# Second stage of a fused attention and gated-FFN kernel: weight jobs issued behind the loads, a semaphore each for queries, keys and V, and a new table of maxima with D1 in the tenth step

## Time and profile before

| | |
|---|---|
| median of 3 runs | 1126.77 us (1122.39 to 1134.81) |
| the profiled execution | 1119.51 us, span of its instructions 1117.7 us |
| busy in the span | PE 93%, DVE 84%, ACT 65%, POOL 42% |
| stage 2 | group 0 starts at 192.3 us, group 15 at 680.0 us, stage 3's first matmul at 709.2 us |

### The profile page before, as it was taken

How to read it: one execution, slowest core, us unless ns; L and a number is a source line. 1 busy time by engine, 2 the same in 40 slices (tenths; PEclk the granted TensorE clock), 3 DMA queues, 4 the chain that set the end, 5 groups by cost and what they waited for, 6 DMA issues and landing times. The chain is left out here.

```text
span 1117.7 us, 18980 instructions
## 1 busy us (share of the span) xinstructions
PE 1039.0 (93%) x6242; PEld 639.5 (57%) x6242; DVE 933.7 (84%) x2162; ACT 722.6 (65%) x1152; POOL 465.6 (42%) x554
## 2 busy tenths in 40 slices
PE   5999987998999999989999999899999999999995
PEld 4788764433344343433444333577778778777874
DVE  6778897887888787878889885579989998998896
ACT  3666655675767666666667668567747766774774
POOL 2566545221111111111121112039946864994686
PEclk9999999999999998999999999899999999999997
DMA  6254862543544544464454343100120011012001
GB/s 214 70 158 137 220 149 78 154 123 64 142 109 109 129 78 97 90 142 109 95 125 94 103 87 106 39 1 0 40 75 1 1 49 66 1 39 76 1 1 38
DMA packets 98584, 95.32 MB, mean 85 GB/s; under 512 B 28030, under 2 KB 80950, under 8 KB 98486
## 3 DMA queue, kind: packets, MB, share of 16 engines
q1 hardware_dynamic: 96854, 93.72, 32.7%
q10 hardware_dynamic: 1632, 0.39, 0.2%
HBM read 72.45 MB, written 21.23 MB: 84 GB/s over the span
## 5 line engine op out<-in xcount | busy, mean ns | idle before, releaser
L896 ACT ACTIVATE pr<-pair 128x1024 f32<-128x1024 f32 (+3 forms) x384 | 296.6, 813 | 168.1 <-PE pair L1017 90.7
L279 DVE CUSTOM_DVE_ANT_0 bank<-bank,sg 128x384 f32<-128x384 f32 (+3 forms) x488 | 231.4, 517 | 73.4 <-PE bank L289 72.1
L1538 PE MATMUL pair<-xc_lo,w_gu 128*128 128x512 f32 x448 | 182.6, 408 | 4.1 <-DVE xc_lo L1374 4.1
L1539 PE MATMUL pair<-xc_hi,w_gu 128*128 128x512 f32 x448 | 176.5, 394 | 0.0
L282 DVE TENSOR_REDUCE mx<-bank 128x1 f32<-128x512 f32 x240 | 150.5, 684 | 6.0 <-PE bank L289 3.7
L1386 DVE SCALAR_TENSOR_TENSOR gate<-pair,sgu,gate 128x512 f32<-128x512 f32 x168 | 124.5, 741 | 27.0 <-PE pair L1539 25.4
L1177 POOL TENSOR_TENSOR yt<-yt,tmp 128x512 f32<-128x512 f32 x96 | 124.2, 1314 | 0.0
L289 PE MATMUL bank<-ks,qs 108*128 108x512 bf16 (+3 forms) x384 | 116.2, 335 | 5.6 <-DMA ks<-in_krows 5.0
L1012 PE MATMUL pair<-s_sb,xin_c 111*128 111x512 bf16 (+3 forms) x384 | 97.8, 338 | 12.0 <-DMA s_sb<-dt 9.2
L289 PE MATMUL bank<-xin_c,s_sb 108*128 108x512 bf16 (+3 forms) x344 | 106.0, 341 | 3.1 <-DMA xin_c<-in_krows 3.0
L1012 PE MATMUL pair<-qs,ks 111*128 111x512 bf16 (+3 forms) x384 | 97.1, 337 | 12.7 <-DMA qs<-dt 11.0
(11 more groups left out here) (122 smaller groups left out, 2166.5 us busy)
## 6 DMA issues: line engine op xcount, KB each, us to landing
stk<-parts SPq DMA_DIRECT2D x16, 768.0 KB, 5.7
zst<-in_z_all SPq DMA_DIRECT2D x24, 448.0 KB, 4.0
sst<-in_w_all SPq DMA_DIRECT2D x24, 448.0 KB, 5.7
xin_c<-in_x SPq DMA_DIRECT2D x32, 256.0 KB, 3.3
s_sb<-stk SPq DMA_DIRECT2D x96, 64.0 KB
xin_c<-stk SPq DMA_DIRECT2D x96, 64.0 KB
qs<-stk SPq DMA_DIRECT2D x96, 64.0 KB
ks<-stk SPq DMA_DIRECT2D x96, 64.0 KB
```

Source lines behind the costliest of these rows:

```text
L279: dve.tensor_tensor_reduce(out=src, in0=src, in1=tri[:, 512 - w:512], scale=1.0, scalar=-3.0e38, op0=ALU.add, op1=ALU.max, accum_out=dst). ...
L896: act.activation(pr[e % 3][:, 2 * p:2 * p + 2, 0:w], pair[p][:, :, 0:w], ACT.Exp, scale=SCALE)\
L1538: pe.matmul(GB[j % 4], w, xc_lo[:, k, :], start=True, stop=False)
L1539: pe.matmul(GB[j % 4], w, xc_hi[:, k, :], start=False, stop=True).then_inc(gu_done, 1)
```

## The change

- SP: in both groups of a pair the job at the group's start is now job s (0 in even, 1 in odd groups), none in group 0. Job 2 is issued in odd groups, behind the load of half 1 and ahead of the load of half 0. ACT converts job 2 at step 2 of the next even group; that of the last pair after the last exponentials, and POOL finishes it after its last group.
- A load is split into 7 DMAs of keys and then 7 of queries, with semaphores `k_in`, `q_in` per slot and half. V has `v_in`, and PE waits for it at step 0 before `pv` of its own group.
- PE waits in the ring for keys of half 1 at the first "u" piece, queries of half 1 at the first early piece, keys of half 0 at the first early piece of the lower half, queries of half 0 at the first head piece.
- The table: 48 pieces, D0, D1, O0, O1 as before, in another order.
- ACT's copy of the upper output of a group waits until O0 of the group before has been transposed.

```diff
-        LOADS = (16 * 15, 16 * 14)
+        LOAD = 16 * 7
...
 PLAN (three rows to a step)
-            "4u 5u 3", "4u", "6u",
-            "5u 2", "3 2", "4u 3",
-            "7u", "7u 3", "2 7u",
-            "O0", "6u 4u", "2 6u",
-            "5u", "6u 7u", "5 4",
-            "6", "4 5", "D0 5",
-            "6", "7 6", "5u",
-            "4", "7", "5",
-            "7 7", "4 6", "",
-            "1", "O1 0", "0",
-            "D1 1", "", "0",
-            "", "1 1", "0",
+            "2 2", "2", "4u",
+            "2 6u", "3 3", "5u 7u",
+            "3 7u", "6u", "5u 5u",
+            "4", "3 7 4", "6u 4u",
+            "4u", "4 4 6", "7",
+            "D0 6", "5 7u", "6u",
+            "5", "7u 7", "5 6",
+            "", "", "4u 7",
+            "5u 5", "6", "O0",
+            "", "", "D1",
+            "1", "", "0 1",
+            "", "O1", "0 0 1 1 0",
...
 SyncE, a group
-                    if s == 1:
-                        half_job(ip, 2)
-                    if not last:
-                        half_job(*((ip, 1), (ip + 1, 0))[s])
+                    if i > 0:
+                        half_job(ip, s)
...
                         load(sp, i + 2, s, 1)
+                    if s == 1:
+                        half_job(ip, 2)
+                    if last is None:
                         sp.wait_ge(s_full[1], full(i, NSTEP - 1, 1))
-                        load(sp, i + 2, s, 0, values=False)
+                        load(sp, i + 2, s, 0)
...
 TensorE, ring
                         if x == of_kind["upper"][0]:
-                            pe.wait_ge(stk_in[1 - s][1], LOADS[1] * (i // 2 + 1 + s))
+                            pe.wait_ge(k_in[1 - s][1], loaded)
+                        if x == of_kind["early"][0]:
+                            pe.wait_ge(q_in[1 - s][1], loaded)
                         if x == of_kind["lower"][0]:
-                            pe.wait_ge(stk_in[1 - s][0], LOADS[0] * (i // 2 + 1 + s))
+                            pe.wait_ge(k_in[1 - s][0], loaded)
+                        if x == of_kind["head"][0]:
+                            pe.wait_ge(q_in[1 - s][0], loaded)
...
 ScalarE, a group
-                        if e == JOB1_AT and s == 1:
-                            convert(ip, 1)
+                        if e == JOB2_AT and s == 0 and i > 0:
+                            convert(ip - 1, 2)
                         if e == JOB_AT:
-                            convert(ip, (0, 2)[s])
+                            convert(ip, s)
```

More of the change, by code:

```diff
@@ L161, in build @@
                 of_hi, of_lo = zip(*[[sb_in(c2)(f"{name}{n}", [P, 512], F32R) for name in ("of_hi", "of_lo")] for n in (0, 1)])
-        stk_in = [[sem(f"stk_in{n}_{b}") for b in range(2)] for n in range(2)]
-        LOADS = (16 * 15, 16 * 14)
+        q_in = [[sem(f"q_in{n}_{b}") for b in range(2)] for n in range(2)]
+        k_in = [[sem(f"k_in{n}_{b}") for b in range(2)] for n in range(2)]
+        v_in = [sem(f"v_in{n}") for n in range(2)]
+        LOAD = 16 * 7
         def load_v(sp, i, s):
-            sp.dma_start(vs[s][:, :, :], vscr[i // GROUPS, :, :, i % GROUPS, :].rearrange("t p w -> p t w"))\
-              .then_inc(stk_in[s][0], 16)
@@ L171, in load, with load_q @@
-        def load(sp, i, s, b, values=True):
+            sp.dma_start(vs[s][:, :, :], vscr[i // GROUPS, :, :, i % GROUPS, :].rearrange("t p w -> p t w")).then_inc(v_in[s], 16)
+        def load_q(sp, i, s, b):
             cols = slice(b * 512, (b + 1) * 512)
[L175 to L181, removed]
@@ L182, in load @@
             g = i % GROUPS
+            src = stk[0, bass.ds(i // GROUPS, 1), bass.ds((i % 2) * 64, 64), bass.ds(g // 2, 1), :, :]\
+                .rearrange("a (j c) k w s -> w c (a j) (k s)", j=GH)
+            for r, part in enumerate((0, 1, 2, 0, 1, 0)):
+                sp.dma_start(qs[s][r * HD:(r + 1) * HD, b, :, :], src[part][:, :, cols]).then_inc(q_in[s][b], 16)
             sp.dma_start(qs[s][96:ROWS_MAX, b, :, :], qrows[bass.ds(g, 1), :, :, cols].rearrange("a p j s -> (a p) j s"))\
-              .then_inc(stk_in[s][b], 16)
+              .then_inc(q_in[s][b], 16)
@@ L185, in load, with load_k @@
+        def load_k(sp, i, s, b):
+            cols = slice(b * 512, (b + 1) * 512)
+            g = i % GROUPS
+            src = stk[1, bass.ds(i // GROUPS, 1), bass.ds((i % 2) * 64, 64), bass.ds(g // 2, 1), :, :]\
+                .rearrange("a (j c) k w s -> w c (a j) (k s)", j=GH)
+            for r, part in enumerate((0, 0, 0, 1, 1, 2)):
+                sp.dma_start(ks[s][r * HD:(r + 1) * HD, :, cols], src[part][:, :, cols]).then_inc(k_in[s][b], 16)
             sp.dma_start(ks[s][96:ROWS, :, cols], krows[bass.ds(g, 1), :, :, cols].rearrange("a p j s -> (a p) j s"))\
-              .then_inc(stk_in[s][b], 16)
@@ L187, in load @@
-            if b == 0 and values:
-                load_v(sp, i, s)
+              .then_inc(k_in[s][b], 16)
+        def load(sp, i, s, b):
+            load_k(sp, i, s, b)
+            load_q(sp, i, s, b)
         m_full, m_free, mx1_done, tri_done = sem("m_full"), sem("m_free"), sem("mx1_done"), sem("tri_done")
@@ L436, in _ @@
                         pairs_stored(sp, 2)
[L437 removed]
+                        load(sp, 0, 0, 0)
                     elif t == 10:
@@ L447, in _ @@
                         load(sp, 1, 1, 13 - t)
+                        if t == 13:
+                            load_v(sp, 1, 1)
                     if t > 2 and t % 2:
@@ L740, in maxima @@
                         if n == 0:
-                            pe.wait_ge(stk_in[0][0], LOADS[0] - 16)
+                            pe.wait_ge(k_in[0][0], LOAD)
+                            pe.wait_ge(q_in[0][0], LOAD)
                         if n == FIRST_EARLY:
-                            pe.wait_ge(stk_in[0][1], LOADS[1])
+                            pe.wait_ge(k_in[0][1], LOAD)
+                            pe.wait_ge(q_in[0][1], LOAD)
                         score(pe, 0, HEAD_ORDER[n], b_a[n % 2], n, banks=2)
@@ L829, in body @@
                 def body(i, s, ip, last):
-                    if s == 1:
-                        half_job(ip, 2)
-                    if not last:
-                        half_job(*((ip, 1), (ip + 1, 0))[s])
-                    else:
+                    if i > 0:
+                        half_job(ip, s)
+                    if last:
                         sp.wait_ge(pv_done, PV0 + NSTEP * i)
@@ L870, in body @@
                 def body(i, s, ip, last):
-                    if s == 1:
-                        job(ip, 1)
+                    if s == 0 and i > 0:
+                        job(ip - 1, 2)
                     pool.wait_ge(m_free, number(i, of_kind["own"][-1]) + 1)
@@ L879, in body @@
                     chain(pool, mx0[:, :, :], 2 * i + 1)
-                    job(ip, (0, 2)[s])
+                    job(ip, s)
                     if not last:
@@ L887, in _ @@
                 groups(body)
+                job((NG - 1) // 2, 2)
             @block.scalar
@@ L899, in copy_o @@
                 def copy_o(i, k):
+                    if k == 0 and i > 0:
+                        act.wait_ge(m_full, number(i, "O0") + 1)
                     act.wait_ge(pv_done, PV0 + NSTEP * i + (FIRST, NSTEP)[k])
@@ L920, in body @@
                             send_d(act, 1 - s, 1, d1_in)
-                        if e == JOB1_AT and s == 1:
-                            convert(ip, 1)
+                        if e == JOB2_AT and s == 0 and i > 0:
+                            convert(ip - 1, 2)
                         if e == JOB_AT:
-                            convert(ip, (0, 2)[s])
+                            convert(ip, s)
                         exps(i, e, 0)
                         exps(i, e, 1)
+                        if last and e == NSTEP - 1:
+                            convert(ip, 2)
                         if e == 0 and i > 0:
@@ L1025, in pv @@
                         pe.wait_ge(ot_done, EXTRA + 2 * i + 1 - qb)
+                    if e == 0:
+                        pe.wait_ge(v_in[s], 16 * (i // 2 + 1))
                     for j in range(GH):
```

5 lines of the change are left out of this document (2 added, 3 removed).

## The result

The changed kernel takes 1095.02 us (median of 4 runs, 1092.29 to 1096.17), the kernel before 1126.88 (1122.39 to 1134.81): ratio 0.9706, 95% interval 0.9649 to 0.9764. The forecast was 1097.0. The profiled execution took 1096.17 us, its span is 1094.0.

What follows compares the result with a forecast made beforehand. PE was taken as the bound, losing 42.7 us to DMA waits and slow clock, DVE second. Gains 19.2, 8.0, 11.1 less costs 9, 3, 1, 0.5, 0.3 gave 24.5 off 1119.5; 2 us added: 1097 us, range 1080 to 1119.

Steps and rivals of the forecast that it cites:

- Length of a group and of the whole: Groups of stage 2 would take about 30.6 us each, and the whole kernel 1097 us.
- Waits for D1, gain 19.2: PE's 20.2 us of waits for `dt` before step 0 would fall to 1 us, with D1 one row earlier.
- what differs is the traffic: D1's DMA needs at most 2.25 us in group 14 but 3.9 to 5.2 elsewhere because of weight jobs and loads.
- Keys of half 1, gain 8.0: PE's 8.0 us of waits at the first "u" piece would go: needed later, loads started 0.84 us earlier.
- Half 0, V and the semaphores: Half 0's keys in odd groups, now behind the weights, would land well before step 3 needs them: no cost.
- Clock, gain 11.1: With PE's idle time gone, the slow clock's 13.7 us would go, except 1 in group 0 and 1.6 for a remaining fall.
- Tail, cost 0.6 a group: With O1 in step 11 and five pieces behind it, DVE becomes the limit at a group's end: 9 us over 15 groups.
- Rest of the table, cost 0.2 a group: DVE's share per step is less even, mostly taken by the ring of three: 3 us in all (0 to 6).
- Weight jobs, cost 1: Job 2 lands 1.3 us before ACT's convert in step 2 of even groups: 1 us in all (0 to 7).
- No tail: Rival: DVE's idle time ahead of O1 makes the tail and table cost near 0: 1085 us, chance 0.20.
- The packets' turn: Rival: D1's DMA stays at 3.9 to 5.2 us whatever is queued, costing 3: 1099 us, chance 0.10 within the forecast's 0.54.
- Slower: Rival: PE's pauses around each group boundary bring the slow clock at all 14: 1147 us, chance 0.09.

Runs made afterwards that it cites:

- the places of the jobs alone: The kernel before with only the weight jobs issued and converted where the change has them; loads, semaphores and table as before: 1093.2 us, ratio 0.972.
- the spread version: The changed kernel with steps 9 to 11 of the table laid out anew, O1 and its scaling pieces spread over them: 1082.3 us, ratio 0.960.
- the order of the load: The kernel before with one edit: each load issues seven DMAs of keys, then seven of queries, on the same semaphore: 1094.6 us, ratio 0.972.
- the run with the lowest, 28.2%: Old table with the new loads and semaphores, jobs issued away from D1, job 2 at the start of even groups and job 0 behind it: 1108.3 us, ratio 0.984.
- all but the table: The changed kernel with the old table (new load order, semaphores and job places kept): 1090.0 us, ratio 0.969.

## Why the prediction was right, and where not

- **Length of a group and of the whole: right.** 30.60 us against 30.6; groups 0 to 14 shorter by 25.7 us against a sum of 24.5; 1095.0 against 1097.0. The forecast for an execution like the profiled one was 1095.0, and the profiled one took 1096.2. The medians differ by 31.9 us, the two profiled executions by 23.3 only: before, the profiled one was 7.3 us under its median, after, it is 1.1 over it. So the slower executions lost the whole of those 7.3 us and not the 5 that I counted on, while the profiled one gained 1.2 us less than forecast. The rows could not tell the first, and that the two together come out within 2 us is luck in part.
- **Waits for D1, gain 19.2: right in size, half right in cause.** All 20.2 us went. The allowed time was worked out as 3.7 us; it is 4.3, since ACT issues 0.52 us behind D1 and not 0.83, and since the tail is longer, so that 4.86 us lie behind D1 and not 4.55. D1 falls to 2.5 to 3.0 (3.5 once), not "towards 2.25". The argument "what differs is the traffic" was right, but I counted only the order of jobs and loads. The alternation inside a load was there in every group and left out, and without it the waits for `dt` fall to 2.1 to 6.0 us with every job where it was. The new table, which the prediction credited with 1.45 us of slack a group, takes 15.8 us of these waits away but gives no time by itself (0.998).
- **Keys of half 1, gain 8.0: right**, none left. But the later place in the table wasn't needed for most of it: the places of the jobs alone leave 0.6 us.
- **Half 0, V and the semaphores, "free": right in the whole change**, but the split is what makes it so. With the table and without the split, PE waits 13.1 us for V. The prediction did not name this condition.
- **Clock, gain 11.1: right.** Groups 1 to 14 show 1.00. Group 0 lost more than counted: 33.56 us at 0.90, before 32.27 at 0.95.
- **Tail, cost 0.6 a group: mis-sized, 0.8 to 1.0.** With A for O1's start, 438.67, PE starts the next group at A + 2.13, not A + 1.95. O1 has been read at A + 1.36, as forecast (439.61 + 0.42), but the second piece behind it frees its bank only with the end of the row below, at 440.64 = A + 1.97, where I had A + 1.78: the short read of the accumulator behind each piece counts. And PE waits 0.26 us for ACT's exponentials in `second(11, 1)`, right ahead of O1:

```profile
438.43 0.11 PEld L1032 LDWEIGHTS pair<-qs,ks 111*128 111x128 bf16 x2 [0.26 <-ACT pr L907]
...
440.50 0.14 DVE L287 DVE_READ_ACCUMULATOR2_ANT mx<- 128x1 f32 x1
```

  Against the A + 1.35 of a tail without DVE that is 0.78, and with the 0.26 it is 1.04. Spreading the tail took 0.98 us off the group.
- **Rest of the table, cost 0.2 a group: wrong in sign, about -0.1**, by one comparison: the spread version has groups of 29.55 against 29.67. With the tail's error the two nearly cancel: 0.8 forecast, 0.86 measured.
- **Weight jobs, cost 1: right.** ACT waits 0.7 us in 2 waits; groups 10 and 12 are 0.4 and 0.3 us longer.
- **The rivals.** "No tail" (1085) was the right size for a version that wasn't there: 1082 to 1088 when the tail is moved. "The packets' turn" put D1 at 3.9 to 5.2 us whatever is queued; with the loads in flight and reordered it takes 2.2 to 3.5. The rule of the Trainium skill behind it ("DMA: Bandwidth & Descriptors", Queues, rings and completion order) says that an engine takes turns between the queue rows, a packet at a time. These runs agree that a small DMA on another queue isn't held until the backlog is gone (in the change D1 lands within 3.5 us while loads still run), but the delay isn't small: 2.2 us become up to 5.3 beside one job. "Slower", with a fall of the clock at each boundary, did not come: none of the waits in the rows above stands in groups 1 to 14.

## What to carry to other kernels

When a small, urgent DMA is late, look at what else the queues do in those microseconds, and at the share of time the packets take for their bytes. Here an edit of the row block that each key load writes took 30 us back, and so did moving the weight jobs from ahead of the loads. The share is a hint and no measure: the places of the jobs gave as much at 31.9% as the order of the load at 30.2%, and the run with the lowest, 28.2%, took 1108.3 us. Run each part of a change alone before crediting any: two of them each gave the whole gain, and the part that looked like the point of it, the table, gave none. A stretch in which TensorE alternates with VectorE is busy in the profile and still loses time; hand such pieces to steps where VectorE is idle.

## What the runs showed of the hardware

- Loads of queries and keys that alternate on the same 16 partitions are slower than the same loads in two orders that don't: the same 96854 packets take 32.7% of the DMA engines' span, and 30.2% in both others; a 1 KB packet of theirs takes 83 ns on average, and 65. D1's DMA beside them takes 2.5 to 5.2 us, and 2.2 to 3.2. All three have a weight job right ahead of each load of half 1. Whether the partitions written or the place of the source does it is open.
- With the jobs elsewhere the same alternating loads take 72 ns a packet, and D1's DMA 2.2 to 3.1 us (two of 4.5).
- A 12 KB DMA on ACT's queue takes 2.2 us in quiet and 4.5 to 5.3 us when it is issued 0.3 us behind 896 KB on SP's queue. With a job's second DMA issued 0.7 us behind it (all but the table, places of the jobs alone) it took 3.9 to 5.2 us, and 2.2 to 2.6 us with 1.3 to 1.8 us between them.
